# Third and fourth layer of a graph network: dense stages merged into one step per block, moments moved into the third pass

## The reference, cut to what matters

```python
# third layer: edge products summed by target node, then a norm over all nodes, then a leaky ReLU
h = segment_sum(concat([x_i, x_j - x_i]) @ W.T + b, dst)
mean = jnp.mean(h, axis=0)
var = jnp.mean(jnp.square(h - mean), axis=0)
h_bn = gamma * (h - mean) * jax.lax.rsqrt(var + BN_EPS) + beta
x = layernorm(x + where(h_bn >= 0, h_bn, 0.01 * h_bn))

# fourth layer: eight relations, attention by target node, self loops added
out = x @ W_self + b_self
for r in range(8):
    h = x @ W[r]; s = h @ a_src[r]; d = h @ a_dst[r]
    e = leaky_relu(s[src] + d[dst], 0.2)
    ... softmax of e over the edges of each dst and relation: alpha
    out = out + segment_sum(alpha * h[src], dst) + bias[r]
x = layernorm(x + out)
```

## Time and profile before

| | us |
|---|---|
| three runs | 8677.41, 8681.29, 8686.11 (median 8681.29) |
| the profiled execution | 8679.14 |
| its span | 8677.3 |
| POOL busy | 6098.5 (70%) |
| DVE busy | 3189.1 (37%) |
| ACT busy | 763.1 (9%) |
| PE busy | 3670.5 (42%) |
| stretch of the third pass used here | 4000 to 5946 |
| moments, third layer's tail, fourth layer's dense part | about 5971 to 6215 |

### The profile page before, as it was taken

How to read it: one execution, slowest core, us unless ns; L and a number is a source line. 1 busy time by engine, 2 the same in 40 slices (tenths; PEclk the granted TensorE clock), 3 DMA queues, 4 the chain that set the end, 5 groups by cost and what they waited for, 6 DMA issues and landing times.

```text
span 8677.3 us, 80150 instructions
## 1 busy us (share of the span) xinstructions
PE 3670.5 (42%) x14706; PEld 2893.5 (33%) x14707; DVE 3189.1 (37%) x6200; ACT 763.1 (9%) x2321; POOL 6098.5 (70%) x6367
## 2 busy tenths in 40 slices
PE   3433434443444444443434333432414454444567
PEld 3333333332222222222222222221214444444554
DVE  3323232333223232322222222224435555555666
ACT  0000000000000000000000000000202222212231
POOL 7777777776777777776777777773277777767715
PEclk6565565665566565565556566665656656666666
DMA  2111111112222222221111111111534444444421
GB/s 57 30 30 30 30 31 29 31 30 49 54 58 56 58 56 57 57 56 32 28 29 28 29 28 29 28 29 41 182 90 118 117 117 110 112 107 112 124 79 33
DMA packets 574051, 520.86 MB, mean 60 GB/s; under 512 B 355868, under 2 KB 355868, under 8 KB 573665
## 3 DMA queue, kind: packets, MB, share of 16 engines
q0 software_dynamic: 200704, 212.34, 14.1%
q1 hardware_dynamic: 344576, 246.02, 10.5%
q10 hardware_dynamic: 28384, 58.61, 1.8%
HBM read 414.92 MB, written 100.74 MB: 59 GB/s over the span
## 4 chain that ended last, share of the span: by engine, by line
POOL 54%; issue 24%; DVE 11%; DVEq 5%; DMA 2%; PE 2%; POOLq 0%; ACT 0%; SPq 0%; ACTq 0%
POOL gat L661 54%; DVEq L299 3%; DVE oh L1448 2%; DMA rel_d<-sum_t 1%; DVE sel L1788 1%; DVE sel L1792 1%; PE p_b L1194 1%; DVE sum_t L1811 1%; DVE toh L1799 0%; DVEq L1780 0%; DVEq L1784 0%; DVE toh L1776 0%; DVE work L1858 0%; DVE dtab L1875 0%; DMA gat<-rel_d,idx 0%
## 5 line engine op out<-in xcount | busy, mean ns | idle before, releaser
L661 POOL DMA_INDIRECT gat<-x_d,idx x3136 | 2964.1, 945 | 1014.4 <-issue 1014.4
L661 POOL DMA_INDIRECT gat<-rel_d,idx x1568 | 1533.3, 978 | 812.5 <-issue 739.0
L661 POOL DMA_INDIRECT gat<-in_x,idx x1568 | 1484.8, 947 | 486.8 <-issue 486.8
L1448 DVE SCALAR_TENSOR_TENSOR oh<-dstf,fine_col,p_b 128x512 f32<-128x512 f32 x1578 | 1108.2, 744 | 393.3 <-issue 363.2
L1080 PE MATMUL p_all<-oh,msg 128*128 128x256 f32 x1568 | 721.4, 640 | 1175.8 <-DVE oh L1448 1175.8
L1080 PE MATMUL p_all<-oh,gat 128*128 128x256 f32 x1568 | 709.4, 631 | 1201.7 <-DMA gat<-x_d,idx 1180.8
L1066 PE MATMUL p_all<-oh,msg 128*66 128x128 f32 x3136 | 703.9, 418 | 1170.4 <-DVE oh L1448 1170.4
L1066 PEld LDWEIGHTS p_all<-oh,msg 128*66 128x66 f32 x3136 | 638.7, 231 | 1231.6 <-issue 1073.8
L1080 PEld LDWEIGHTS p_all<-oh,gat 128*128 128x128 f32 x1568 | 482.7, 323 | 1423.0 <-issue 1116.9
L1080 PEld LDWEIGHTS p_all<-oh,msg 128*128 128x128 f32 x1568 | 489.5, 327 | 1398.3 <-issue 1082.5
L1551 DVE TENSOR_TENSOR sum_t<-sum_t,p_all 64x128 f32 x784 | 222.5, 284 | 1301.2 <-PE p_all L1080 1154.2
(11 more groups left out here) (283 smaller groups left out, 3510.4 us busy)
## 6 DMA issues: line engine op xcount, KB each, us to landing
he_d<-gat ACTq DMA_DIRECT2D x196, 288.0 KB, 2.2
ea<-he_d SPq DMA_DIRECT2D x196, 288.0 KB
ea<-in_edge_attr SPq DMA_DIRECT2D x196, 256.0 KB, 2.7
gat<-x_d,idx POOLq DMA_INDIRECT x3136
drow<-dst_d SPq DMA_DIRECT2D x196, 256.0 KB, 3.6
rel_d<-sum_t SPq DMA_DIRECT2D x14, 2016.0 KB, 7.1
gat<-in_x,idx POOLq DMA_INDIRECT x1568
gat<-rel_d,idx POOLq DMA_INDIRECT x1568
```

The lines of the kernel that those rows point to most:

```text
L661: nc.gpsimd.indirect_dma_start(out=gat[:, q, s, :] if width == HROW else got[:, q, s, :], out_offset=None, in_=table, in_offset=bass.Indir ...
L1448: return vec.scalar_tensor_tensor(out=oh[:, u, cut, :], in0=bc(dst.unsqueeze(2), P, S // 2, W), scalar=fine_col[0:P, bass.ds(at, 1)], in1= ...
```

## The change

- The two dense stages become one loop of 14 steps. In a step DVE does the leaky step of block b+2, the new rows of block b+1 and the relation part of block b; PE and ACT have the matching order; SP stores rows b+1, loads old rows b+3 and stores relations b (`relations_io` in place of `dense_io(3)` and `dense_io(4)`).
- PE turns the new rows from `yo`, where DVE has written them; they are still stored to `x3_d` (the last layer reads them), but the fourth layer's 14 loads are gone.
- The leaky step writes `stage` in place, since `xt` now holds the turned rows. PE's turned hidden rows go to the PSUM banks `p_sum`, the turned rows to `p_tr` bank 0, the scores to `p_tr` bank 1.
- The scores of two tiles come from one product: `sdw` is 128 x 32 with the second copy of the weights in the other rows and columns, zeros elsewhere (4 products per block for 7).
- ACT copies tiles 0, 1, 2, 4, 5, 6 out, with the root of block b+1 between the third and the fourth; DVE copies tile 3.
- The staging blocks `hst` move from `sum_t` to the starts of `trip_s` and `trip`, with store semaphores of their own (`s_relst`). SP issues the store of block b and then waits for that of block b-1.
- The split of the tables waits until the store of block 12 has landed, the clearing of `trip` until that of block 13 has.
- Two `bn_stats` per block (448 nodes each, the last shorter) run in step j = 5 of the third pass; `layers34` only aggregates.

The core of the diff:

```diff
             def relations_io():
+                def keep_rows(u, it, b):
+                    wait_for(sp, s_y[3], b + 1)
+                    sp.dma_start(rows(Y[3], b), yo[:, u, :, :]).then_inc(s_yst[u], 16)
+                    wait_for(sp, s_yst[u], it * 16 + 16 * (1 + NI * stored[3]))
+                    sp.sem_inc(s_yfree[3], 1)
+                def keep_relations(u, b):
+                    wait_for(sp, s_y[4], b + 1)
+                    wait_for(sp, s_act[4], b + 1)
+                    sp.dma_start(rel_d[bass.ds(b * BC * R, BC * R), :].rearrange("(t p r) c -> p t (r c)", p=W, r=R),
+                                 hst[u].rearrange("p t r c -> p t (r c)")).then_inc(s_relst[u], 16)
+                def relations_kept(u, it):
+                    wait_for(sp, s_relst[u], it * 16 + 16)
+                    sp.sem_inc(s_yfree[4], 1)
...
+                def step(it, u, b):
+                    keep_rows(1 - u, it + u, b + 1)
+                    wait_for(sp, s_xfree[3], b + 4)
+                    load(1 - u, b + 3)
+                    keep_relations(u, b)
...
+                with sp.Fori(1, NI - 2) as it:
+                    for u in range(2):
+                        step(it, u, it * 2 + u)
+                        relations_kept(1 - u, it - 1 + u)
...
             # ACT
+                def step(u, b, more=2):
+                    if more > 1:
+                        scale_shift(u, b + 2)
+                    wait_for(act, s_yfree[4], b + 1)
+                    some_tiles(u, b, (0, 1, 2))
+                    if more:
+                        square_root(3, b + 1, 0, 1)
+                    k, count = some_tiles(u, b, (4, 5, 6))
...
+                    if more:
+                        turned(1 - u, b + 1)
...
             # PE
+                        products4(u, b)
+                        turn_rows3(1 - u, b + 1)
+                        turn_hidden(u, b + 2)
...
             # DVE
+            def moments(b, last):
+                for k in range(2):
+                    width = TAIL - HB if last and k else HB
+                    ins = vec.bn_stats(out=bn[:, bass.ds(b * 2 + k, 1), :].rearrange("d a c -> d (a c)"),
+                                       in_=sum_t[0:D, nodes(b, width, k * HB)])
+                ch(ins)
...
+                if j == 5:
+                    moments(b, isinstance(b, int) and b == NB - 1)
...
             def layers34():
-                dve.wait_ge(s_mid[2], NB + 2)
                 ch.start()
-                for c in range(25):
-                    ch.add(vec.bn_stats(out=bn[:, c, :], in_=sum_t[0:D, c * (N // 25):(c + 1) * (N // 25)]))
-                ch.wait()
...
+                def new_rows(u, it, b):
...
+                    ch(vec.tensor_tensor(ya[:, :, :], bank(p_sum, u, D), xs[:, u, :, :], ALU.add))
+                    dve.sem_inc(s_xfree[3], 1)
+                    wait_for(dve, s_tr[4], b + 1)
+                    layer_norm(3, b, u)
...
+                        leaky(u, b + 2)
+                        new_rows(1 - u, it + u, dve.snap(b + 1))
+                        relations(u, b)
...
+                dve.wait_ge(s_yfree[4], NB + 1)
                 ch.start()
                 ch(vec.memset(dtab_v[1], 0.0))
...
+                dve.wait_ge(s_yfree[4], NB + 2)
                 ch(vec.memset(trip_flat, 0.0))
```

More of the change, by code:

```diff
@@ L210, in program @@
         s_yst = [sem(f"s_yst{u}") for u in range(2)]
+        s_relst = [sem(f"s_relst{u}") for u in range(2)]
         s_yfree = {n: sem(f"s_yfree{n}") for n in (0, 1, 3, 4, 5)}
@@ L519, in _ @@
             pass_io(2)
[L520 to L521 removed]
+            relations_io()
             def dst_row(u, g):
@@ L588, in _ @@
                         refill(2, q, it, src_p)
-                for n in (2, 3, 4):
-                    dense_io(n)
+                dense_io(2)
+                relations_io()
                 first_indices(3, key_d)
@@ L825, in layers34 @@
+                for b in range(2):
+                    scale_shift(b, b)
+                square_root(3, 0, 0, 1)
+                turned(0, 0)
+                with act.Fori(0, NI - 1) as it:
+                    for u in range(2):
+                        step(u, act.snap(it * 2 + u))
+                step(0, NB - 2, 1)
+                step(1, NB - 1, 0)
                 act.wait_ge(s_zero, 2)
@@ L1713, in layers34 @@
                 dve.sem_inc(s_bn, 1)
-                def leaky(it, u, b):
-                    wait_reg(dve, s_act[3], b + 1)
-                    vec.scalar_tensor_tensor(out=xt[0:D, u, :], in0=stage[0:D, u, :], scalar=0.01,
-                                             in1=stage[0:D, u, :], op0=ALU.mult, op1=ALU.max).then_inc(s_mid[3], 1)
-                two_step(dve, leaky, finish(3, p_b))
-                ch.start()
-                dve.wait_ge(s_y[3], NB)
-                for u in range(2):
-                    ch(vec.memset(hst[:, u, :, :, D + 1:HROW], 0.0))
@@ L1726, in layers34, with leaky @@
-                dve.sem_inc(s_zero, 1)
-                with dve.Fori(0, NI) as it:
+                for u in range(2):
+                    ch(vec.memset(hst[u][:, :, :, D + 1:HROW], 0.0))
+                dve.sem_inc(s_zero, 1)
+                def leaky(u, b):
+                    wait_for(dve, s_act[3], b + 1)
+                    vec.scalar_tensor_tensor(out=stage[0:D, u, :], in0=stage[0:D, u, :], scalar=0.01,
+                                             in1=stage[0:D, u, :], op0=ALU.mult, op1=ALU.max).then_inc(s_mid[3], 1)
@@ L1728, in layers34 @@
+                for b in range(2):
+                    leaky(b, b)
+                new_rows(0, 0, 0)
+                with dve.Fori(0, NI - 1) as it:
                     for u in range(2):
                         b = dve.snap(it * 2 + u)
-                        ch.start()
-                        wait_reg(dve, s_sd, b + 1)
-                        for k in range(2):
-                            ch.add(vec.tensor_copy(sd[:, k:BT:2, :], sd_bank[k]))
-                        ch.wait()
-                        dve.sem_inc(s_xfree[4], 1)
```

186 lines of the change are left out of this document (114 added, 72 removed).

## The result

Four runs of the changed kernel took 8606.23 to 8611.69 us, median 8607.33, beside 8683.70 for the kernel before on the same chip: 0.9914 of its time, 95% interval 0.9902 to 0.9927, or 76.4 us less. I had said 8588, in a range of 8574 to 8614. The direction and the place are right; of the 92.8 us that I had summed for the profiled execution, the two profiled executions show 72.2 (span 8677.3 to 8605.1). The 20.6 us that are missing are what the experiments are about.

A forecast was written before the change was run, and what follows sets the result against it. Bound in POOL's standstill: DVE's chain in the third layer, single-file relation stores in the fourth. First gather moves from 6215.26 to 6122.5, 92.8 us off 8679.14, giving 8586.3; plus 2.15, 8588 us, range 8574 to 8614.

The forecast's parts named there:

- The gap: POOL's 262.5 us standstill from the third pass's last gather to the first relation gather; forecast to become about 170 us.
- the moments: The norm's 25 instructions on DVE, 14.60 us, leave POOL's standstill; two at 0.584 us stay; gain 13.4 us.
- the start: The first merged step begins at 5986.0: block 0's rows ready at 5984.0, then 2.0 us for turning and copying.
- The merged step: One step of the merged third and fourth layer takes 9.4 us, out of a summed 9.2 to 9.9.
- the ring: Merged step's closed chain between ACT's turned copies of successive blocks, through scaling, DVE's leaky step to new rows, turning; 9.4 us.
- SP's order: SP's three transfers per merged step hide with 1.5 us to spare; a relation store has 9.4 us, needs 7.1.
- rival B: In merged steps the row store is held behind the earlier relation store: 10.9 us a step, 18 us more, 8606; chance 0.23.
- C: Merged steps lose part of the overlap (DVE's relation work or tiles): 11.8 to 13.5 us each, 8617 to 8637; chance 0.09.
- D's single file: Merged steps don't overlap, both old blocks run in a row: 19.2 us each, 8706 in all, slower; chance 0.02.
- The end: After steps 0 to 11: last relation store issued at +13.8 us, landed at +22.5, first gather at +23.7, or 6122.5.
- Behind the first gather: Nothing edited from first relation gather to the end; 2462 us stays within 6 us; chance of a gain lost there 0.01.
- A: The case as summed: merged steps of 8.9 to 9.9 us, 8576 to 8601 with the uncertain end; chance 0.62.

The follow-up runs named there:

- the kernel with twenty waits: The changed kernel plus twenty long-satisfied waits (ten instructions) on DVE ahead of its wait for the last relation stores; time ratio 0.9907 to the kernel before.

## Why the prediction was right, and where it was off

- *The gap as the place, the moments, the start.* Right. Moments 13.4 us forecast, 12.5 to 14.4 measured by two runs. First merged step at 5988.2 for 5986.0; the third pass ended 2.5 us later in that execution, less than the 8 us by which its end differs between the two profiles of before.
- *The merged step, 9.4 us.* The mechanism was right at the higher clock and the size off in all: 12 steps took 6106.97 - 5988.2 = 118.8 us, 9.90 each, 6.0 us too many. The term that failed is the sentence that lists PE's 22 instructions among what "lies beside the ring"; where the clock was 0.67 they were the ring. I had weighed the clock for the turning only, where it decides 0.46 us, and not for the seven products of 64x512 and the four of the scores; with these PE's list fills 9.15 of 10.2 us at 0.67. The earlier trace rows had the warning: in the old fourth layer PE was busy 20.78 of 24.00 us at 0.93. DVE's chain came out at 9.15 and 9.47 us by turns at the higher clock, near the low end of my 9.2 to 9.9; the old blocks too took 6.3 and 6.6 us by turns, and I had read the 6.3 alone.
- *SP's order and rival B.* SP hid, as summed, and the wait for the row store costs nothing (177.9 against 178.6 us). C is out as well: DVE waits for ACT and, through it, for PE, not PE for DVE's relation work. D's single file did not come. But neither did the sign that some relation stores go out before the one before has landed: they went out 9.2 to 10.4 us apart, the last two 7.2, and each had landed before the next; my own 9.4 and 7.1 had left no room for it.
- *The end, 23.7 us.* 25.3 from the turned copy of block 12 to the first gather, out of two misses that partly cancel. The last store went out at +17.0 us, not +13.8, since the last block's scores and products on PE, which the sum left out, take 6.4 us behind its turned copy. And it landed in 7.1 us, where I had taken some 8.7, as the shift copies went out 2.4 us behind it.
- *Behind the first gather, "nothing is edited".* This is the step that failed outright. I had given 0.01 to a gain lost there, and a change of more than 6 us was my sign of being wrong outright; the stretch grew by 10.8 us. Of these 8.7 are the three returns of DVE's loop. The other 2 are not accounted for, and lie within the 6 us by which the stretch differs among the kernels with cheap returns (2459.2 to 2465.4). Nothing in that loop was edited, but its place was. The first fetched rows were taken 21.2 us after the first gather, not 23, and these 5 us of delay did hide: in the kernel with twenty waits they are taken as late, and its stretch is 2459.2 us, no longer than before.

In sum 2.2 + 6.0 + 1.6 + 10.8 = 20.6 us, the whole of the miss. That the range held is luck: 8607.33 lies outside A's 8576 to 8601, the case that I had forecast. The range reached it only because it took in B, which did not happen, and whose price of 18 us is near that of two causes that I had not priced.

## What to carry to other kernels

When stages with different loads on TensorE are merged, sum its whole list at both levels of the clock and compare each with the ring of the other engines. The clock of the parts was no guide here: 0.50 and 0.93 in the old layers, 0.67 in most of the merged steps. An edit ahead of a long loop moves the loop's code: count each engine's instructions up to the loop's head before and after, and look in the profile for idle time ahead of its first instruction that nothing ends; a few waits that are long satisfied can move it back. A change that frees a transfer earlier has to be followed to what it then flies beside.

## What the runs showed of the hardware

- The return of DVE's loop cost 4.3 to 4.8 us in every profile with the loop's head at instruction 5379, 5381, 5382 or 5389, and 6.8 to 7.9 us in every profile with it at 5371.
- In the merged stage of the changed kernel the granted clock was 0.82 to 0.97 in four of eleven steps and 0.67 in six, with the same work in each; in its second profile it was 0.93 in one and 0.67 to 0.68 in nine. The step at 0.67 shown by the microsecond ran at 1.2 GHz for about two thirds of its time and at 2.4 GHz for the rest. It was 0.50 in nine of eleven steps when a part of the products was cut, and 0.82 to 0.98 in six of eleven with the scores doubled.
- A 2 MB store landed in 7.1 us with two copies of 0.4 MB each (64 partitions of 6272 and 6208 bytes) issued 2.4 us or more behind it, in 9.5 us with the copies 1.4 and 2.0 us behind (second profile of before), and in 11.1 to 11.5 us with them 0.1 to 0.9 us behind. In the first profile of before, with the copies 0.3 us ahead of it and 0.2 behind, it took 10.93.
